# Products of probabilities and values in pairs of steps, with four buffers of probabilities

## Chip, cores and metric

One core of a Trainium2 chip. The metric is the device time of one execution in microseconds. Engines are named as the profile names them: PE is TensorE (matmuls; PEld are its weight loads), DVE is VectorE, ACT is ScalarE, POOL is GpSimd, SP is SyncE, which issues the DMAs.

## The reference

Attention with a bias by relative position that is added after the softmax, two layer norms with residuals, and a layer of 32 small experts of which each token takes its best 4. Four batches of 512 tokens with 128 features, 16 heads of 8.

```
q, k, v = split_heads(x @ Wq), split_heads(x @ Wk), split_heads(x @ Wv)
attn = softmax(einsum('bhqd,bhkd->bhqk', q, k) * e ** -0.5) + bias
x = layernorm(x + layernorm(einsum('bhqk,bhkd->bhqd', attn, v)) * gamma + beta)
sim = (x @ hasher_w.T) @ keys.T
vals, idx = top_k(sim, 4);  w = softmax(vals)
out = sum_k w[k] * (silu(x @ values_down[idx[k]]) @ values_up[idx[k]])
x = layernorm(x + out * scale)
```

## The kernel before

**Rounds and steps.** The kernel runs rounds t = 0 to 4 (2 and, where more are needed, a loop over the middle ones). Round t has the attention of batch t and, from round 1 on, the norms and the experts of batch t - 1; from round 2 on also the last `up` products of batch t - 2. Round 4 is a tail without attention. A round has 16 steps u: four groups of four heads, and in each group four blocks of 128 keys (kc = u % 4). Each engine has its own program, written by hand in a fixed order, and the engines meet at semaphores.

**A step on TensorE** (`round_`, lines 1186 to 1216). Four scores (`scores`, line 1007, bf16, into one of three banks `st_ps`), four maxima matmuls (`maximum_scores`, line 996, into one of two banks `sm_ps`, for the heads seven positions ahead), one product of probabilities and values (`values`, line 1020), and jobs. A product is four matmuls in float32 with 32 columns of weights each, on four column tiles side by side; the trace has eight instructions for it, since each float32 matmul is two passes. It accumulates over the four key blocks of a group in `ov_ps`. In step u stands the product of step u - 1; that of step 15 stands in step 0 of the next round. The order is: score 0 (and 1), maxima m0, scores to 2, maxima m1, the product, maxima m2, jobs "before", score 3, maxima m3, jobs "behind".

**Jobs** (table `JOBS`). Turnings of the shifts for the next group (`shift0` to `shift3`; `shift0` is that of the next round and stands in step 14), of outputs (`o0` to `o3`), of the normed rows (`x1t`, step 5), the expert similarities (`sim`, step 6), the turning of the expert weights `w_tok` (`wt`, step 9), eight `down` and eight `up` products of the experts.

**VectorE** takes the row maximum of each maxima matmul (line 747) in the same order, and between them the normalisation of a head group in steps 1, 5, 9 and 15 (lines 766 and 768), norm statistics in steps 1 to 4, `hid` from step 7 on (line 801) and the ranking of the experts in steps 6 to 9. A maxima matmul waits for the reduction two before it, because there are two banks.

**ScalarE** does the Exp of each score (line 656) into `probs`, of which there are two buffers, so a step's first Exp waits for the product two steps back. It also copies `ov_ps` to `o_sb` after the last product of a group.

**GpSimd** does its work in one queue: copies of values, the norms, the splits of the maxima into three bf16 parts (lines 424 to 431), and the multiplication of `hid` by the expert weights (`weigh`, line 464). The weights `w_rows` reach it from `w_tok` by way of `w_t`, a write to DRAM and eight broadcast reads on SP's queue. The split for `shift0` stands in it behind the sixth of eight multiplications.

Of the kernel before, what the change touches and what calls it, by code (L numbers as in the profile page):

```python
# [5 lines left out]
def bass_postln_attention_product_key_ffn(nc, x, w_q, w_k, w_v, rel_table, gamma, beta,  # L6
# [18 lines left out]
    ALU, ACT, AX = mybir.AluOpType, mybir.ActivationFunctionType, mybir.AxisListType  # L25

    B, S, E = x.shape
    H = rel_table.shape[1]
    D = E // H
    P = 128  # L30
    C = S // P
    J = 4
    G = H // J
    U = G * C
# [11 lines left out]
    LAST = rel_table.shape[0] - 1  # L46
    NWIN = S
    TILE = 32
    EPS_ATTENTION, EPS_LN = 1e-3, 1e-5

    def constant_from(h):

        return min(max(-(-(LAST - S + HPB + HPB * h) // HPB), 0), H)
# [7 lines left out]
    with ctx:  # L61
        def sb(name, shape, dt=F32):
            return ctx.enter_context(nc.sbuf_tensor(name, shape, dt))

        def pb(name, shape, dt=F32):
            return ctx.enter_context(nc.psum_tensor(name, shape, dt))

        def sem(name):
            return ctx.enter_context(nc.semaphore(name))
# [18 lines left out]
        v_all = sb("v_all", [P, C, H, B, D])  # L88
        v_cur = sb("v_cur", [P, C, H, TILE])
        q_stack, k_stack = sb("q_stack", [P, H, S], BF16), sb("k_stack", [P, H, S], BF16)  # L90
# [2 lines left out]
        shift_parts = sb("shift_parts", [P, P // (J * C), J * C], BF16)  # L93
        shift_res = sb("shift_res", [P, J * C])
        shift_rows = sb("shift_rows", [PARTS * J * C, P], BF16)
        probs = sb("probs", [P, 2, J, S])
        o_sb = sb("o_sb", [P, S])
        rsum = sb("rsum", [P, C, J])
        attn = sb("attn", [P, C, E])
        bias_t = sb("bias_t", [P, 2, S])  # L100
        bias_v = sb("bias_v", [P, C, H, B, D])

        z = sb("z", [P, C, E])
# [11 lines left out]
        w_rows = sb("w_rows", [P, FJ, S])  # L115
        tanh_sb = sb("tanh_sb", [P, 3, S])
        hid = sb("hid", [P, FJ, S])
        y, y_out = sb("y", [P, C, E]), sb("y_out", [P, C, E])


        st_ps = pb("st_ps", [P, 3, S])
# [25 lines left out]
        scores_ready, probs_ready, pv_done = sem("scores_ready"), sem("probs_ready"), sem("pv_done")  # L147
# [15 lines left out]
        def maxima_of(u, more):  # L163

            return [(u + LEAD, c) for c in range(C) if more or u + LEAD < U]
# [26 lines left out]
        def here(n, attention, experts, more, late):  # L192

            return (late if n[:2] == "up" else attention if n in OWN else experts) and (more or n != "shift0")
# [42 lines left out]
        def score_bank(k):  # L237


            return 1 if k == U * J - 1 else k % 3  # L240
# [34 lines left out]
        def bias_banks(g):  # L275


            return [(st_ps[:, 0, :], st_ps[:, 2, :]), (st_ps[:, 1, :], st_ps[:, 0, :])][(g - CG) % 2]
# [5 lines left out]
        def is0(t):  # L284
            return isinstance(t, int) and t == 0
# [285 lines left out]
        def _(act):  # L571
# [77 lines left out]
            def exp(t, u, j):  # L649

                n = t * U + u
                act.wait_ge(scores_ready, J * n + j + 1)
                if j == 0 and not (is0(t) and u < 2):

                    act.wait_ge(pv_done, n - 1)
                nc.scalar.activation(probs[:, u % 2, j, :], st_ps[:, score_bank(u * J + j), :], ACT.Exp,  # L656
                                     scale=SCORE_SCALE).then_inc(probs_ready, 1)

            def o_copy(t, g, in_round):
# [294 lines left out]
        def _(pe):  # L954
# [32 lines left out]
            def maximum_scores(t, pos, c):  # L987

                n, h = t * U + pos, pos % U
                k = C * n + c  # L990
                if pos % J == 0 and c == 0:
                    pe.wait_ge(stack_loaded[pos // J % G], 32 * (t + pos // U) + 32)
                if not (is0(t) and pos == 0 and c < 2):

                    pe.wait_ge(max_ready, k - 1)
                nc.tensor.matmul(sm_ps[:, c % 2, :], q_stack[0:SHIFT_ROW, h, c * P:(c + 1) * P],  # L996
                                 k_stack[0:SHIFT_ROW, h, :], start=True, stop=True).then_inc(sm_ready, 1)

            def scores(t, u, j):

                n, g, kc, k = t * U + u, u // C, u % C, u * J + j
                if j == 0 and kc == 0:
                    pe.wait_ge(shift_loaded[g], 16 * t + 16)
                if not (is0(t) and k < 3):

                    pe.wait_ge(probs_ready, J * n + j + 1 - scores_since(k))
                nc.tensor.matmul(st_ps[:, score_bank(k), :], k_stack[:, g * J + j, kc * P:(kc + 1) * P],  # L1007
                                 q_stack[:, g * J + j, :], start=True, stop=True).then_inc(scores_ready, 1)

            def values(t, u):  # L1010

                n, g, kc = t * U + u, u // C, u % C
                if kc == 0:
                    pe.wait_ge(v_ready, t * G + g + 1)
                    if not (is0(t) and g == 0):

                        pe.wait_ge(o_copied, t * G + g)
                pe.wait_ge(probs_ready, J * n + J)
                for j in range(J):
                    i = nc.tensor.matmul(ov_ps[j * TILE:(j + 1) * TILE, :], v_cur[:, kc, g * J + j, :],  # L1020
                                         probs[:, u % 2, j, :], start=(kc == 0), stop=(kc == C - 1))
                i.then_inc(pv_done, 1)

            def turn(dst, src, idn):
# [107 lines left out]
            for kc in range(C):  # L1132
                i = nc.tensor.matmul(st_ps[:, 2, 0:CG * J * B * D], rel_t[:, LAST:LAST + P],
                                     v_all[:, kc, 0:CG * J].rearrange("p h b d -> p (h b d)"),
                                     start=(kc == 0), stop=(kc == C - 1))
# [12 lines left out]
            for g in range(CG, G):  # L1148
                if g >= CG + 2:
                    pe.wait_ge(bias_copied, g - CG - 1)  # L1150
                n = constant_from((g + 1) * J - 1) + 1
                for kc in range(C):
                    for j in range(J):
                        h = g * J + j
                        window = bass.AP(rel_t, S - 1 - HPB * h + (P // H) * kc, [[pitch, P], [HPB, n], [-1, HPB]])
                        i = nc.tensor.matmul(bias_banks(g)[0][j * TILE:(j + 1) * TILE, 0:n * HPB],
                                             v_all[:, kc, h].rearrange("p b d -> p (b d)"), window, start=(kc == 0), stop=(kc == C - 1))
# [18 lines left out]
            def round_(t, attention, experts, more, late):  # L1176
                kind = (attention, experts, more, late)

                def jobs(half):
                    for name in half:  # L1180
                        if here(name, *kind):
                            misc(t, name, kind)

                for u in range(U):
                    before, behind = JOBS.get(u, ([], []))

                    if not attention and u == 0:

                        before, behind = behind, before
                    todo = maxima_of(u, more) if attention else []  # L1190

                    def maxima(k):
                        for pos_c in todo[k:k + 1]:
                            maximum_scores(t, *pos_c)

                    def score(*heads):
                        for j in heads:
                            if attention:
                                scores(t, u, j)

                    spread = not any(here(n, *kind) and n[:2] in ("do", "up") for n in JOBS.get(u - 1, ([], []))[1])
                    score(*range(1 + spread))
                    maxima(0)
                    score(*range(1 + spread, 3))
                    maxima(1)
                    if u and attention:
                        values(t, u - 1)
                    elif u == 0 and experts:
                        values(t - 1, U - 1)
                    maxima(2)  # L1210
                    jobs(before)
                    score(3)
                    maxima(3)
                    jobs(behind)

            rounds(pe, round_)
            for j in range(FJ):
                up(B - 1, j, B + 1)
# [22 lines left out]
```

## Time and profile before

| | |
|---|---|
| time, median of 3 runs | 367.4 us (366.94 to 367.63) |
| span of the profiled execution | 365.1 us |
| busy: PE, DVE, ACT, POOL | 304.6, 239.0, 189.2, 119.1 us |
| TensorE clock granted, mean | 0.922 |
| round 0 from its first product to the first product of round 1 | 51.4 to 99.1 us |
| turning of `w_tok` in rounds 1, 2, 3 | 135.90, 210.18, 283.75 us |

A timeline row has the start and the duration in us, the engine, the line, the operation with its output and inputs, and in brackets how long the engine was idle before it and what ended that. A row with "x4" is four instructions of one kind in a row. Matmuls overlap, so TensorE is best read from start to start.

### The profile page before, as it was taken

The numbers are of one execution on the slowest core, as the hardware profiler recorded it, in microseconds if no ns is written. First come the engines' busy times: TensorE is split into PE (matmuls) and PEld (weight loads), VectorE is DVE, ScalarE is ACT, GpSimd is POOL, SyncE is SP. The second block draws the span as 40 slices with busy tenths as digits, with TensorE's granted clock in tenths as the row PEclk, the third lists the DMA queues.
The fourth block names the chain that finished last, engine by engine and source line by source line (L and its number), as shares of the span: only waits on it lengthen the run. The fifth ranks groups of instructions, "written<-read, shape, count | busy, mean of one in ns | idle before, by whom it ended". The sixth has DMA issues, their size and how long they took to land. (4 is left out here: it accounts for less than half of the span.)

```text
span 365.1 us, 4853 instructions
## 1 busy us (share of the span) xinstructions
PE 304.6 (83%) x1603; PEld 132.9 (36%) x1627; DVE 239.0 (65%) x525; ACT 189.2 (52%) x370; POOL 119.1 (33%) x185
## 2 busy tenths in 40 slices
PE   5858989999998999839999999299999998185771
PEld 2524323232232433214544333145543227142661
DVE  0737797888898798806788988157789222656123
ACT  2634366777776667625466768155567890024000
POOL 8834000011057111450565105513660044440111
PEclk9969999999999999969999999789999999759556
DMA  5487942298112021332021212430000122001220
GB/s 147 96 257 184 309 87 68 75 301 277 40 29 66 5 64 66 110 127 68 3 65 33 65 52 103 137 81 2 1 27 6 45 102 94 0 29 50 103 86 30
DMA packets 32983, 31.83 MB, mean 87 GB/s; under 512 B 6670, under 2 KB 27326, under 8 KB 32958
## 3 DMA queue, kind: packets, MB, share of 16 engines
q1 hardware_dynamic: 32958, 31.52, 29.0%
q8 instruction: 13, 0.21, 0.3%
q14 instruction: 12, 0.10, 0.1%
HBM read 20.57 MB, written 10.78 MB: 86 GB/s over the span
## 5 line engine op out<-in xcount | busy, mean ns | idle before, releaser
L747 DVE TENSOR_REDUCE neg_max<-sm_ps 128x1 f32<-128x512 f32 x256 | 167.4, 685 | 61.5 <-PE sm_ps L996 60.4
L656 ACT ACTIVATE probs<-st_ps 128x512 f32<-128x512 f32 x256 | 137.3, 601 | 46.1 <-PE st_ps L1007 32.2
L996 PE MATMUL sm_ps<-k_stack,q_stack 96*128 96x512 bf16 x256 | 100.2, 393 | 9.4 <-DVE neg_max L747 4.0
L1007 PE MATMUL st_ps<-q_stack,k_stack 128*128 128x512 bf16 x232 | 79.7, 388 | 0.9 <-ACT probs L656 0.7
L1020 PE MATMUL ov_ps<-probs,v_cur 128*32 128x512 f32 x512 | 68.3, 605 | 1.0 <-ACT probs L656 1.0
L996 PEld LDWEIGHTS sm_ps<-k_stack,q_stack 96*128 96x128 bf16 x256 | 24.9, 98 | 100.4 <-DVE neg_max L747 78.7
L464 POOL TENSOR_TENSOR hid<-hid,w_rows 128x512 f32<-128x512 f32 x26 | 33.0, 1268 | 80.9 <-DMA w_rows<-w_dram 80.8
L1041 PE MATMUL si_ps<-up_sb,hid 128*128 128x128 f32 x256 | 39.1, 310 | 10.0 <-DVE hid L939 6.0
L1041 PEld LDWEIGHTS si_ps<-up_sb,hid 128*128 128x128 f32 x256 | 36.4, 219 | 14.0 <-POOL hid L464 5.0
L1007 PEld LDWEIGHTS st_ps<-q_stack,k_stack 128*128 128x128 bf16 x256 | 25.6, 100 | 29.4 <-ACT probs L656 10.4
L1096 PE MATMUL mi_ps<-x_t,down_sb 128*128 128x512 f32 x48 | 24.6, 593 | 0.0
L801 DVE SCALAR_TENSOR_TENSOR hid<-tanh_sb,mi_ps 128x512 f32<-128x512 f32 x24 | 16.3, 680 | 10.6 <-ACT tanh_sb L687 10.6
L687 ACT ACTIVATE tanh_sb<-mi_ps 128x512 f32<-128x512 f32 x24 | 14.4, 600 | 13.6 <-PE mi_ps L1096 13.6
L439 POOL COPY v_cur<-v_all 128x128 f32<-128x128 f32 x16 | 4.5, 291 | 49.8 <-PE ov_ps L1020 49.8
L1020 PEld LDWEIGHTS ov_ps<-probs,v_cur 128*32 128x32 f32 x512 | 10.1, 108 | 23.7 <-issue 18.7
L424 POOL CAST shift_parts<-neg_max 128x16 bf16<-128x16 f32 x16 | 3.2, 197 | 41.5 <-DVE neg_max L747 41.5
L573 ACT ACTIVATE shift_rows<-mi_ps 48x128 bf16<-48x128 bf16 x16 | 4.3, 271 | 22.6 <-PE mi_ps L1025 22.5
L1025 PE MATMUL mi_ps<-ident_bf,shift_parts 128*128 128x128 bf16 x16 | 3.6, 226 | 14.2 <-POOL shift_parts L431 14.0
L939 DVE TENSOR_TENSOR hid<-hid,w_rows 128x512 f32<-128x512 f32 x6 | 4.2, 693 | 16.5 <-DMA w_rows<-w_dram 16.5
L573 ACT ACTIVATE x_t<-si_ps 128x512 f32<-128x512 f32 x4 | 2.4, 597 | 20.1 <-PE si_ps L1025 20.1
L573 ACT ACTIVATE o_sb<-ov_ps 128x512 f32<-128x512 f32 x16 | 9.6, 599 | 5.9 <-PE ov_ps L1020 5.7
L1096 PE MATMUL st_ps<-x_t,down_sb 128*128 128x512 f32 x16 | 9.6, 758 | 0.2 <-DVE hid L801 0.2
(126 smaller groups left out, 268.0 us busy)
## 6 DMA issues: line engine op xcount, KB each, us to landing
w_rows<-w_dram SPq DMA_DIRECT2D x32, 256.0 KB
stack_dram<-parts SPq DMA_DIRECT2D x18, 384.0 KB, 4.7
q_stack<-stack_dram SPq DMA_DIRECT2D x16, 288.0 KB
k_stack<-stack_dram SPq DMA_DIRECT2D x16, 288.0 KB
stack_dram<-parts SPq DMA_DIRECT2D x6, 288.0 KB, 5.0
x_sb<-L_attn_x SPq DMA_DIRECT2D x4, 256.0 KB, 3.5
out<-y_out SPq DMA_DIRECT2D x4, 256.0 KB, 2.5
stack_dram<-parts SPq DMA_DIRECT2D x6, 96.0 KB, 2.1
```

Of the source, the lines that this page charges most:

```text
L439: nc.gpsimd.tensor_copy(v_cur[:, :, g * J:(g + 1) * J, 0:D], v_all[:, :, g * J:(g + 1) * J, t, :]).then_inc(v_ready, 1)
L464: nc.gpsimd.tensor_tensor(hid[:, j], hid[:, j], w_rows[:, j], ALU.mult).then_inc(weighed, 1)
L573: return nc.scalar.activation(dst, src, ACT.Copy, scale=scale)
L656: nc.scalar.activation(probs[:, u % 2, j, :], st_ps[:, score_bank(u * J + j), :], ACT.Exp, scale=SCORE_SCALE).then_inc(probs_ready, 1)
L687: nc.scalar.activation(tanh_sb[:, j % 3, :], down_bank(t, j), ACT.Tanh, scale=0.5).then_inc(act_step, 1)
L747: nc.vector.tensor_reduce(neg_max[:, g % 2, col:col + 1], sm_ps[:, c % 2, :], AX.X, ALU.max, negate=True).then_inc(max_ready, 1)
L801: nc.vector.scalar_tensor_tensor(out=hid[:, j], in0=tanh_sb[:, j % 3, :], scalar=1.0, in1=down_bank(t, j), op0=ALU.add, op1=ALU.mult).then ...
L996: nc.tensor.matmul(sm_ps[:, c % 2, :], q_stack[0:SHIFT_ROW, h, c * P:(c + 1) * P], k_stack[0:SHIFT_ROW, h, :], start=True, stop=True).then ...
L1007: nc.tensor.matmul(st_ps[:, score_bank(k), :], k_stack[:, g * J + j, kc * P:(kc + 1) * P], q_stack[:, g * J + j, :], start=True, stop=True ...
L1020: i = nc.tensor.matmul(ov_ps[j * TILE:(j + 1) * TILE, :], v_cur[:, kc, g * J + j, :], probs[:, u % 2, j, :], start=(kc == 0), stop=(kc == ...
L1041: i = nc.tensor.matmul(si_ps[:, c * P:(c + 1) * P], hid[:, j, c * P:(c + 1) * P], up_sb[:, j, :], start=(j == 0 and c == 0), stop=(j == FJ ...
L1096: i = nc.tensor.matmul(down_bank(t, j), down_sb[:, j * NJ:(j + 1) * NJ, :], x1_t[:], start=True, stop=True)
```

## The change

Products of two steps stand together in the even steps: in step u those of steps u - 2 and u - 1, in step 0 those of steps 14 and 15 of the round before. Odd steps have none. `probs` gets four buffers, so that the first Exp of a step waits for the product four steps back. For its room `bias_t`, used before round 0 only, becomes a part of `hid`.

```
+    AV_STEPS = 2
-        probs = sb("probs", [P, 2, J, S])
+        probs = sb("probs", [P, 2 * AV_STEPS, J, S])
-        bias_t = sb("bias_t", [P, 2, S])
+        bias_t = hid[:, 0:2, :]
...
-                if j == 0 and not (is0(t) and u < 2):
-                    act.wait_ge(pv_done, n - 1)
-                nc.scalar.activation(probs[:, u % 2, j, :], st_ps[:, score_bank(u * J + j), :], ACT.Exp,
+                if j == 0 and not (is0(t) and u < 2 * AV_STEPS):
+                    act.wait_ge(pv_done, n - 2 * AV_STEPS + 1)
+                nc.scalar.activation(probs[:, u % (2 * AV_STEPS), j, :], st_ps[:, score_bank(u * J + j), :], ACT.Exp,
...
-                                         probs[:, u % 2, j, :], start=(kc == 0), stop=(kc == C - 1))
+                                         probs[:, u % (2 * AV_STEPS), j, :], start=(kc == 0), stop=(kc == C - 1))
...
-                    if u and attention:
-                        values(t, u - 1)
-                    elif u == 0 and experts:
-                        values(t - 1, U - 1)
+                    if u % AV_STEPS == 0:
+                        for step in range(AV_STEPS, 0, -1):
+                            if u and attention:
+                                values(t, u - step)
+                            elif u == 0 and experts:
+                                values(t - 1, U - step)
```

TensorE, steps 1 and 2 of round 0, before: `sm_ps` is written by maxima matmuls, `st_ps` by scores, `ov_ps` by the product.

```order
L996 MATMUL sm_ps<-k_stack,q_stack 128x512
L1020 MATMUL ov_ps<-probs,v_cur 32x512 x4
L996 MATMUL sm_ps<-k_stack,q_stack 128x512
L1007 MATMUL st_ps<-q_stack,k_stack 128x512
L996 MATMUL sm_ps<-k_stack,q_stack 128x512
L1007 MATMUL st_ps<-q_stack,k_stack 128x512 x2
L996 MATMUL sm_ps<-k_stack,q_stack 128x512
L1007 MATMUL st_ps<-q_stack,k_stack 128x512
L996 MATMUL sm_ps<-k_stack,q_stack 128x512
L1020 MATMUL ov_ps<-probs,v_cur 32x512 x4
```

The same place in the changed kernel, whose lines stand one further:

```order
L997 MATMUL sm_ps<-k_stack,q_stack 128x512 x2
L1008 MATMUL st_ps<-q_stack,k_stack 128x512
L997 MATMUL sm_ps<-k_stack,q_stack 128x512
L1008 MATMUL st_ps<-q_stack,k_stack 128x512 x2
L997 MATMUL sm_ps<-k_stack,q_stack 128x512
L1008 MATMUL st_ps<-q_stack,k_stack 128x512
L997 MATMUL sm_ps<-k_stack,q_stack 128x512
L1021 MATMUL ov_ps<-probs,v_cur 32x512 x8
```

The product of step 1 is gone, so that m1 and m2 stand side by side, and step 2 has two.

TensorE around the turning of `w_tok`, from m1 of step 9 on, before:

```order
L996 MATMUL sm_ps<-k_stack,q_stack 128x512
L1020 MATMUL ov_ps<-probs,v_cur 32x512 x4
L996 MATMUL sm_ps<-k_stack,q_stack 128x512
L1025 MATMUL mi_ps<-ident_bf,shift_parts 128x128
L1007 MATMUL st_ps<-q_stack,k_stack 128x512
L996 MATMUL sm_ps<-k_stack,q_stack 128x512
L1025 MATMUL si_ps<-ident,w_tok 128x128
```

In the changed kernel:

```order
L997 MATMUL sm_ps<-k_stack,q_stack 128x512 x2
L1026 MATMUL mi_ps<-ident_bf,shift_parts 128x128
L1008 MATMUL st_ps<-q_stack,k_stack 128x512
L997 MATMUL sm_ps<-k_stack,q_stack 128x512
L1026 MATMUL si_ps<-ident,w_tok 128x128
```

The product of step 8 is no longer ahead of the turning; it stands in step 10.

## Rows read from the trace of the kernel before

**Rows 1.** The page: busy time of engines; the costliest groups, TensorE's products.

```profile
PE 304.6 (83%) x1603; PEld 132.9 (36%) x1627; DVE 239.0 (65%) x525; ACT 189.2 (52%) x370; POOL 119.1 (33%) x185
...
L1020 PE MATMUL ov_ps<-probs,v_cur 128*32 128x512 f32 x512 | 68.3, 605 | 1.0 <-ACT probs L656 1.0
```

**Rows 2.** Timeline, round 1: turning of w_tok, GpSimd's wait, TensorE's wait.

```profile
135.90 0.30 PE L1025 MATMUL si_ps<-ident,w_tok 128*128 128x128 f32 x1 [0.16 <-DVE w_tok L895]
...
158.29 1.26 POOL L464 TENSOR_TENSOR hid<-hid,w_rows 128x512 f32<-128x512 f32 x1 [2.28 <-DMA w_rows<-w_dram]
...
160.80 0.27 PE L1025 MATMUL mi_ps<-ident_bf,shift_parts 128*128 128x128 bf16 x1 [6.53 <-POOL shift_parts L431]
```

**Rows 3.** Timeline, tail: VectorE's variance, GpSimd's last multiplication and its norm.

```profile
306.25 0.38 DVE L786 BATCH_NORM_AGGREGATE mv<-stats 128x2 f32<-128x6 f32 x4
...
310.81 1.26 POOL L464 TENSOR_TENSOR hid<-hid,w_rows 128x512 f32<-128x512 f32 x1 [1.32 <-DMA w_rows<-w_dram]
...
312.15 0.23 POOL L448 TENSOR_SCALAR veps<-mv 128x4 f32<-128x4 f32 x1
```

**Rows 4.** Timeline, round 0, a plain step: TensorE, then VectorE.

```profile
83.57 0.61 PE L1020 MATMUL ov_ps<-probs,v_cur 128*32 128x512 f32 x4
84.12 0.39 PE L996 MATMUL sm_ps<-k_stack,q_stack 96*128 96x512 bf16 x1
84.34 0.38 PE L1007 MATMUL st_ps<-q_stack,k_stack 128*128 128x512 bf16 x1
...
85.89 0.39 PE L996 MATMUL sm_ps<-k_stack,q_stack 96*128 96x512 bf16 x1
86.21 1.06 PE L1020 MATMUL ov_ps<-probs,v_cur 128*32 128x512 f32 x8
87.21 0.39 PE L996 MATMUL sm_ps<-k_stack,q_stack 96*128 96x512 bf16 x1
...
84.54 2.48 DVE L747 TENSOR_REDUCE neg_max<-sm_ps 128x1 f32<-128x512 f32 x4 [0.61 <-PE sm_ps L996]
87.64 2.54 DVE L747 TENSOR_REDUCE neg_max<-sm_ps 128x1 f32<-128x512 f32 x4 [0.61 <-PE sm_ps L996]
```

**Rows 5.** Timeline, round 1, VectorE in steps 2 to 4.

```profile
106.94 3.08 DVE L747 TENSOR_REDUCE neg_max<-sm_ps 128x1 f32<-128x512 f32 x5
110.60 2.48 DVE L747 TENSOR_REDUCE neg_max<-sm_ps 128x1 f32<-128x512 f32 x4 [0.57 <-PE sm_ps L996]
113.34 0.87 DVE L778 BATCH_NORM_STATS2 stats<-z 128x6 f32<-128x128 f32 x4 [0.25 <-POOL z L528]
```

**Rows 6.** Timeline, rounds 1 and 2, steps 15, 1, 3, 4 and 8.

```profile
164.09 0.69 DVE L747 TENSOR_REDUCE neg_max<-sm_ps 128x1 f32<-128x512 f32 x1 [1.44 <-PE sm_ps L996]
...
165.75 0.39 PE L996 MATMUL sm_ps<-k_stack,q_stack 96*128 96x512 bf16 x1
...
172.75 0.69 DVE L747 TENSOR_REDUCE neg_max<-sm_ps 128x1 f32<-128x512 f32 x1 [0.40 <-PE sm_ps L996]
...
174.08 0.39 PE L996 MATMUL sm_ps<-k_stack,q_stack 96*128 96x512 bf16 x1
...
182.03 1.34 DVE L747 TENSOR_REDUCE neg_max<-sm_ps 128x1 f32<-128x512 f32 x2 [0.64 <-PE sm_ps L996]
...
183.58 0.39 PE L996 MATMUL sm_ps<-k_stack,q_stack 96*128 96x512 bf16 x1
...
188.19 1.29 DVE L747 TENSOR_REDUCE neg_max<-sm_ps 128x1 f32<-128x512 f32 x2
...
204.02 0.39 PE L996 MATMUL sm_ps<-k_stack,q_stack 96*128 96x512 bf16 x1
...
205.07 0.69 DVE L747 TENSOR_REDUCE neg_max<-sm_ps 128x1 f32<-128x512 f32 x1
```

**Rows 7.** Timeline, round 0, VectorE in steps 5 and 15 to 0.

```profile
64.92 3.14 DVE L747 TENSOR_REDUCE neg_max<-sm_ps 128x1 f32<-128x512 f32 x5
...
98.81 0.69 DVE L747 TENSOR_REDUCE neg_max<-sm_ps 128x1 f32<-128x512 f32 x1 [0.23 <-PE sm_ps L996]
```

## The prediction

> **What bounds the kernel now.** The page comes first: TensorE is busy 83% of the span and VectorE 65%, and the products of probabilities and values are 512 of TensorE's instructions, eight to a step [rows 1]. A total does not say what sets the end, so the second view is the timeline at the two places where work ends that everything else waits for. In the last step but one of a round with experts, TensorE sits idle 6.53 us until GpSimd has split the next shifts. GpSimd could not, for its queue stood behind a multiplication by `w_rows` that waited for a DMA, and that DMA goes back to the turning of `w_tok` in step 9, at 135.90 [rows 2]. So from step 9 to the split the time is that of DMAs: what TensorE does in steps 10 to 14 costs nothing, up to those 6.53 us. In the tail it is the same: the mean and variance of the last batch are there at 306.63, but GpSimd takes them at 312.15, behind the multiplication that the last-but-one slice of `w_rows` released [rows 3]. **The path** is thus round 0 from step 1, round 1 to step 9, then steps 15 and 0 to 9 of rounds 2 and 3. The rest hangs on those three `w_tok`.
>
> What limits a step on the path? I read a plain one of round 0 in the timelines of both engines [rows 4]. TensorE issues the step's second maxima matmul (call it m1) at 85.89, the product at 86.21, the third one (m2) at 87.21; VectorE starts on m2 at 87.64, 0.43 later. Reductions in a row start 0.60 apart ((2.48 - 0.69)/3). The next m1 may go only when the reduction two before it has ended, since there are two banks: 0.60 + 0.69 after VectorE took m2, and 0.05 of semaphore. The loop is 1.32 + 0.43 + 0.60 + 0.69 + 0.05 = 3.09, which is the distance from one m2 to the next (84.12 to 87.21). It is a chain through both engines, and the product stands inside it: while it runs VectorE idles 0.61 [rows 4].
>
> **The change, part by part.**
>
> *The even steps, each with one more product.* One product is two passes of four matmuls. From its start to m2 it is 1.00 (86.21 to 87.21), from its second pass to m2 0.55 (83.57 to 84.12), so the passes are 0.45 apart, and of the 1.00 two passes are 0.91 and 0.09 stands behind them [rows 4]. No row shows two products in a row. I take 0.91 for the second, two passes without the 0.09; the bounds are 0.88 (four pitches of 0.22, that of two bf16 matmuls of 512 columns, 84.12 to 84.34) and 1.10 (it starts afresh, 1.00 and 0.10 ahead of it). m2, and with it VectorE, comes 0.91 later. Even steps on the path: 2, 4, ... 14 in round 0, and 0, 2, 4, 6, 8 in each of rounds 1 to 3, so 7 + 15 = 22, or +20.0 us.
>
> *Cover.* Where VectorE has other work queued when m2 comes, part of the 0.91 is hidden. In step 2 of round 1 it runs behind until 106.94 and starts on m2 some 0.60 later, so 0.37 is hidden; in step 4 of round 1 it is held by a statistic that waits for GpSimd's `z`, 0.46; in step 4 of rounds 2 and 3 m1's reduction starts at 188.19 and the next at 188.80, where m2 issued about 188.20 was ready at 188.62, so 0.2 each; in step 8 of all three rounds m2 goes at 204.02 and is taken at 205.07 only, so 0.63 each [rows 5, 6]. With 0.05 each in step 2 of rounds 2 and 3: 0.37 + 0.46 + 0.4 + 1.9 + 0.1 = 3.2 us. Net of the even steps: +16.8.
>
> *The odd steps, without a product.* m2 follows m1 at once, but it has to wait for the reduction of m0. The step is then VectorE's: four reductions 0.60 to 0.61 apart, 2.45 in place of 3.09, a gain of 0.64 and not of the product's 1.00. That holds in steps 1, 3, 7, 11 and 13 of round 0: 3.2 us. In steps 5 and 9 the normalisation of a head group stands between the reductions, and VectorE has five in a row with no idle time behind it, so nothing is gained; in step 15 only the 0.23 of idle time ahead of the next step, with the overlap of 0.07: 0.3 [rows 7]. In round 1, step 1 is full of normalisation and statistics up to 106.94 (nothing), step 3 gives back its 0.57 and the overlap (0.64), step 5 waits for GpSimd's norm (nothing), and in steps 7 and 9 VectorE works without a gap on reductions, `hid` and the ranking (nothing) [rows 5]. In rounds 2 and 3, m2 could go 0.74 after m0's reduction starts: in step 15 at 164.83 and not 165.75, in step 1 at 173.49 and not 174.08 (0.59), in step 3 at 182.77 and not 183.58 (0.81) [rows 6]. Of the 0.92 of step 15 I count 0.6, since m3 then waits for m1's reduction, which ends late (bounds 0.26 and 0.92). Steps 5, 7 and 9 give nothing, as in round 1. Together 3.5 + 0.64 + 2 x 2.0 = 8.1 us.
>
> *Edits with no price.* Four buffers of probabilities: the Exp of a step waits for a product four steps back. With pairs it was done one or two steps before, so ScalarE is not held, nor SP and GpSimd. `bias_t` in the place of `hid`: one is used before round 0, the other first written in round 1. The product of step 8 goes from ahead of `w_tok`'s turning to behind it; that turning waits for VectorE's `w_tok`, not for the product. The copies of `ov_ps` stand one to four steps, as before, behind the last product of a group. Steps 10 to 14 change by 1 to 2 us, inside the 6.53 of [rows 2]; if that cover were gone, they would add 3 us in all.
>
> **The sum.** +16.8 - 8.1 = +8.7. The profiled execution: 365.1 + 8.7 = 373.8. The median lies 2.3 above the span, so 367.4 + 8.7 = 376.1 us.
>
> **A rule beside the rows.** The product runs on column tiles of 32, all else on the whole array, and a change between the two costs: 0.09 behind the product, and 0.32 from m1 to it where the pitch is 0.22, so 0.10 ahead [rows 4]. The Trainium skill, TensorEngine Tiling (Array Packing), section Key Properties, says it: "Changing tiling mode (not just tile) drains the TensorE". The trace agrees, with 0.19 a product. By that rule alone half the switches go and the kernel gets faster, which is the first rival; its price comes from the rows.
>
> **The rivals.**
> *TensorE is the limit, and each switch saved is time saved.* For it: TensorE is the busiest engine [rows 1], and two of the odd steps of rounds 2 and 3 give back most of what its work is shorter by [rows 6]. The path now holds 15 + 10 + 11 + 11 = 47 products at 1.00 + 0.10; it would hold 22 pairs at 1.10 + 0.91 (three products move behind `w_tok`). That is 51.7 less 44.2, so 367.4 - 7.5 = 359.9 us. It decides if m2 can go right behind m1 in an odd step, that is if m0's reduction has ended by then. Against it: m0 goes 0.44 ahead of m1, and its reduction ends 0.43 + 0.69 after its issue, 0.46 after the place of m2; and in the plain step VectorE idles while TensorE multiplies.
> *A seam between the products.* If the second starts afresh it costs 1.10 and not 0.91, 22 times 0.19: +4.2, 380.3 us. Against: the second pass of a product follows the first at 0.45, its weights loaded beneath, and the next product is on the same four tiles.
> *VectorE catches up better.* If the even steps of rounds 1 to 3 hide another 0.3 each (15 times) since VectorE arrives with more queued from the odd step, 4.5 is saved: 371.6 us. Against: it is never more than two reductions behind, by the two banks.
> *The path is elsewhere,* in transfers that do not go back to `w_tok`: then nothing changes, 367.4 us. Against: the turning of `w_tok` waited 0.16 for VectorE alone, and GpSimd's multiplication for the DMA of what it made [rows 2].
>
> **How the numbers follow.** Chances: the forecast (372.5 to 379) 0.70, the seam (379 to 382) 0.08, the better cover (369 to 372.5) 0.10, the path elsewhere 0.04, TensorE the limit 0.08. Measurements of this kernel tell about 0.2% from no change. The range takes in the forecast, most of the better cover and part of the seam: 370.5 to 380.5. Faster 0.08, the same 0.04, slower 0.88.
>
> **What would show it.** In the timeline after: 16 instructions of the product in a row, m2 1.91 behind their start in even steps; in plain pairs of round 0, products 6.4 apart (2 x 3.09 + 0.91 - 0.64) where two steps took 6.18; VectorE idle 1.5 before m2 of an even step and not at all in the odd one; the idle time of TensorE until the shift split near 6 us again; from `w_tok` to the end the same time as now. The three turnings of `w_tok` should come about 5.3, 7 and 8.7 later. I am wrong if the pairs of round 0 are no further apart than 6.18, or if the reductions of the odd steps do not follow each other without a gap.

## The result, and the profile after

The changed kernel takes **374.19 us** (median of 4 runs, 372.99 to 375.05) beside 367.51 for the kernel before (4 runs). The ratio is **1.019, 95% interval 1.015 to 1.022**: slower by 6.7 us. The forecast was 376.1 and its range 370.5 to 380.5. The profiled execution took 372.99, its span is 371.2.

These are the page's busy times and the two groups that changed most, of the kernel after (a row: busy us, mean ns, then idle time just before and what ended most of it):

```profile
PE 303.3 (82%) x1604; PEld 134.6 (36%) x1627; DVE 238.0 (64%) x525; ACT 189.9 (51%) x370; POOL 118.9 (32%) x185
...
L748 DVE TENSOR_REDUCE neg_max<-sm_ps 128x1 f32<-128x512 f32 x256 | 166.1, 683 | 68.5 <-PE sm_ps L997 67.7
...
L997 PE MATMUL sm_ps<-k_stack,q_stack 96*128 96x512 bf16 x256 | 99.7, 391 | 21.5 <-DVE neg_max L748 14.8
```

And the same two groups on the page of the kernel before:

```profile
L747 DVE TENSOR_REDUCE neg_max<-sm_ps 128x1 f32<-128x512 f32 x256 | 167.4, 685 | 61.5 <-PE sm_ps L996 60.4
...
L996 PE MATMUL sm_ps<-k_stack,q_stack 96*128 96x512 bf16 x256 | 100.2, 393 | 9.4 <-DVE neg_max L747 4.0
```

The two busiest engines have no more to do: TensorE 303.3 us against 304.6, VectorE 238.0 against 239.0 [rows 1]. But VectorE waits 7 us longer for TensorE's maxima, and TensorE's maxima wait 11 us longer for VectorE (14.8 against 4.0, the part that VectorE's reductions end). Each engine now waits for the other at different times. That is a loss without a culprit in the totals; it is seen only in the order of things within a pair of steps. The timeline of the kernel after, round 0, steps 2 to 4, TensorE first:

```profile
52.59 0.39 PE L997 MATMUL sm_ps<-k_stack,q_stack 96*128 96x512 bf16 x1
52.91 1.92 PE L1021 MATMUL ov_ps<-probs,v_cur 128*32 128x512 f32 x16
54.77 0.39 PE L997 MATMUL sm_ps<-k_stack,q_stack 96*128 96x512 bf16 x1
...
57.14 0.39 PE L997 MATMUL sm_ps<-k_stack,q_stack 96*128 96x512 bf16 x1 [0.20 <-DVE neg_max L748]
...
59.25 1.06 PE L1021 MATMUL ov_ps<-probs,v_cur 128*32 128x512 f32 x8
```

then VectorE:

```profile
43.34 10.43 DVE L748 TENSOR_REDUCE neg_max<-sm_ps 128x1 f32<-128x512 f32 x17 [0.25 <-PE sm_ps L997]
55.20 4.97 DVE L748 TENSOR_REDUCE neg_max<-sm_ps 128x1 f32<-128x512 f32 x8 [1.43 <-PE sm_ps L997]
61.53 1.29 DVE L748 TENSOR_REDUCE neg_max<-sm_ps 128x1 f32<-128x512 f32 x2 [1.37 <-PE sm_ps L997]
```

m2 comes 1.86 behind the start of the two products (52.91 to 54.77), where it came 1.00 behind one [rows 4]: the second product costs 0.86. VectorE idles 1.43 before it, then does eight reductions with no gap, through the whole odd step; that is why the odd step gives nothing like 1.00 back. The pair takes 6.34 us (52.91 to 59.25) where two steps took 6.18.

The other reading is TensorE's wait before the shift split, and the turning of `w_tok` in rounds 1 and 2:

```profile
139.55 0.30 PE L1026 MATMUL si_ps<-ident,w_tok 128*128 128x128 f32 x1 [0.16 <-DVE w_tok L896]
```

```profile
164.42 0.27 PE L1026 MATMUL mi_ps<-ident_bf,shift_parts 128*128 128x128 bf16 x1 [4.00 <-POOL shift_parts L432]
```

```profile
215.45 0.30 PE L1026 MATMUL si_ps<-ident,w_tok 128*128 128x128 f32 x1 [0.16 <-DVE w_tok L896]
```

The turning is 3.65 later in round 1 (135.90 before [rows 2]), 5.27 in round 2, 6.08 in round 3. From the turning to the split it is 24.87 us, where it was 24.90: that stretch swallowed its pairs, and the wait at its end shrank from 6.53 [rows 2] to 4.00. By stretch, with the start of the first score matmul and the turnings as marks:

| us | before | after |
|---|---|---|
| start to first score | 47.93 | 46.98 |
| first score to turning 1 | 87.97 | 92.57 |
| turning 1 to split 1, turning 2 to split 2 | 24.90, 25.24 | 24.87, 24.43 |
| split 1 to turning 2, split 2 to turning 3 | 49.38, 48.33 | 51.03, 49.95 |
| turning 3 to end | 81.35 | 81.37 |

The path, that is the second and fourth lines, grew by 4.60 + 1.65 + 1.62 = 7.9 us. The span grew by 6.1, because this execution had its first score 0.95 sooner and one stretch of transfers 0.8 shorter. The first says little: two kernels below that have the four buffers and no pair before step 12 of round 1 had their first score at 47.17 and 48.49, on either side of the kernel before. For the second no run tells whether the change has a part in it.

### The profile page after: what moved, and what is told of

Same layout as the page of the kernel before. It is cut to its first block and busy times, and to the rows that moved or that the text cites. A ratio compares the mean times of both kernels' runs of the same rounds, so it can differ in the third digit from the quotient of the medians.

```text
span 371.2 us, 4852 instructions
## 1 busy us (share of the span) xinstructions
PE 303.3 (82%) x1604; PEld 134.6 (36%) x1627; DVE 238.0 (64%) x525; ACT 189.9 (51%) x370; POOL 118.9 (32%) x185
## 5 line engine op out<-in xcount | busy, mean ns | idle before, releaser
L997 PE MATMUL sm_ps<-k_stack,q_stack 96*128 96x512 bf16 x256 | 99.7, 391 | 21.5 <-DVE neg_max L748 14.8
L1021 PE MATMUL ov_ps<-probs,v_cur 128*32 128x512 f32 x512 | 61.6, 598 | 0.0
L1021 PEld LDWEIGHTS ov_ps<-probs,v_cur 128*32 128x32 f32 x512 | 13.4, 109 | 29.4 <-issue 17.8
L574 ACT ACTIVATE o_sb<-ov_ps 128x512 f32<-128x512 f32 x16 | 9.6, 598 | 17.4 <-PE ov_ps L1021 17.4
```

Source lines behind the costliest of these rows:

```text
L574: return nc.scalar.activation(dst, src, ACT.Copy, scale=scale)
```

## The experiments

All are compared with runs of the kernel before on the same chip. A plain step or pair below is one of round 0 with nothing but reductions on VectorE.

**Only the buffers.** Does the loss come from the four buffers or from `bias_t` in the place of `hid`? The kernel before with those edits alone (`AV_STEPS` is 2):

```
-        probs = sb("probs", [P, 2, J, S])
+        probs = sb("probs", [P, 2 * AV_STEPS, J, S])
...
-        bias_t = sb("bias_t", [P, 2, S])
...
+        bias_t = hid[:, 0:2, :]
...
-                if j == 0 and not (is0(t) and u < 2):
-                    act.wait_ge(pv_done, n - 1)
-                nc.scalar.activation(probs[:, u % 2, j, :], ...
+                if j == 0 and not (is0(t) and u < 2 * AV_STEPS):
+                    act.wait_ge(pv_done, n - 2 * AV_STEPS + 1)
+                nc.scalar.activation(probs[:, u % (2 * AV_STEPS), j, :], ...
```

> The four buffers of probabilities and bias_t in hid alone; the products stand as before, one in each step. Theory (VectorE is starved while two products run): buffers cost nothing, 367.4 us as before, within 0.3%. Rival (the memory, the longer distance between Exp and product, or the alias costs): 370 us or more, a part of the 6.7 us.

366.82 us (10 runs) against 367.08 (25 runs), ratio 1.000, interval 0.998 to 1.003. The buffers are free; the loss is all in where the products stand.

**One product in the even steps, none in the odd ones.** The changed kernel without the first product of each pair, to split the sum into its two halves:

```
                     if u % AV_STEPS == 0:
-                        for step in range(AV_STEPS, 0, -1):
-                            if u and attention:
-                                values(t, u - step)
-                            elif u == 0 and experts:
-                                values(t - 1, U - step)
+                        if u and attention:
+                            values(t, u - 1)
+                        elif u == 0 and experts:
+                            values(t - 1, U - 1)
```

Two more edits, not shown, go with it: a sum over key blocks begins at the first product that is left, and each product counts as two at its semaphore.

> The changed kernel with the first product of each pair left out (half of the products of probabilities and values are not computed): even steps have one product, odd steps none. It splits the sum. Theory: against the changed kernel it is faster by what the second product costs net of cover, 22 x 0.86 less 3.2 = 16 us, so 358 us; against the kernel before it is faster by what the odd steps give back, 8 to 9 us, and not by the 25 products x 1.10 us = 27 us that are gone from the path. Rival (TensorE's own work is the limit): 340 us.

The median of ten runs is 364.3 us, ratio 0.992 (0.989 to 0.994): by the medians the 358 us expected were missed. The profiled run is the fastest, 359.3. The others lie between 361.4 and 367.5 at a mean granted clock of 0.893 to 0.916, where this one had 0.924 and the kernel before 0.917 to 0.930. On the three stretches of the path its clock was 1.00, 0.96 and 0.94 and that of the kernel before 1.00, 0.96 and 0.96, so the trace of this run is what is compared; what follows rests on this one execution. Its TensorE in the same steps:

```profile
52.76 1.06 PE L1021 MATMUL ov_ps<-probs,v_cur 128*32 128x512 f32 x8
53.76 0.39 PE L997 MATMUL sm_ps<-k_stack,q_stack 96*128 96x512 bf16 x1
...
56.13 0.39 PE L997 MATMUL sm_ps<-k_stack,q_stack 96*128 96x512 bf16 x1 [0.21 <-DVE neg_max L748]
...
58.24 1.06 PE L1021 MATMUL ov_ps<-probs,v_cur 128*32 128x512 f32 x8
```

and its VectorE:

```profile
54.18 4.96 DVE L748 TENSOR_REDUCE neg_max<-sm_ps 128x1 f32<-128x512 f32 x8 [0.57 <-PE sm_ps L997]
```

With half of all products gone a plain pair takes 5.48 (52.76 to 58.24), 0.70 less than two steps before, and VectorE again has eight reductions in a row. A whole product out of the odd step is worth 0.70 there, not 1.00. The path's three stretches are 84.09, 48.18 and 47.15, so **emptying the odd steps gave back 3.9 + 1.2 + 1.2 = 6.3 us**; and from there to the changed kernel, **the second products cost 8.5 + 2.9 + 2.8 = 14.1**. If TensorE were the limit, this kernel would have come near 340.

**Pairs only where time was said to be free.** The kernel before with the four buffers, and with pairs in steps 12 and 14 of rounds 1 to 3 alone (steps 11 and 13 have no product then):

```
+                    paired = experts and attention
+                    if paired and u in (12, 14):
+                        values(t, u - 2)
+                        values(t, u - 1)
+                    elif paired and u in (11, 13):
+                        pass
+                    elif u and attention:
...
```

> Pairs only in steps 12 and 14 of rounds 1 to 3, which lie behind the turning of w_tok; all other steps as before. Theory (the path ends at w_tok, the DMAs and GpSimd set the time from there to the shift split): 367.4 us, the same, and TensorE's wait before the split changes by under 1 us. Rival (a step costs what it takes wherever it stands): 6 of 22 pairs, +2 us or more.

367.37 us against 367.08, ratio 1.000 (0.998 to 1.003): the stretch behind `w_tok` hides its pairs. What was missed is the size of what it hides:

```profile
161.14 0.26 PE L1026 MATMUL mi_ps<-ident_bf,shift_parts 128*128 128x128 bf16 x1 [4.68 <-POOL shift_parts L432]
```

It was 6.53 [rows 2]. A pair takes 8.22 here (its products start at 145.99 and 154.21) where two steps took 7.40 (138.08 to 145.48 in the kernel before), so two pairs spent 1.64 of it. What a plain pair of round 0 costs (6.34 less 6.18) does not hold in these steps: each also has two matmuls of the experts' first layer (`down`) on TensorE, and the `hid` made of them on VectorE, and the odd step without a product is no shorter for it. VectorE now waits 0.94 ahead of m2 and still 0.44 in the next gap, as the rows of these two engines in the first of the two pairs show:

```profile
145.99 1.92 PE L1021 MATMUL ov_ps<-probs,v_cur 128*32 128x512 f32 x16
...
154.21 1.92 PE L1021 MATMUL ov_ps<-probs,v_cur 128*32 128x512 f32 x16
```

```profile
148.27 1.29 DVE L748 TENSOR_REDUCE neg_max<-sm_ps 128x1 f32<-128x512 f32 x2 [0.94 <-PE sm_ps L997]
150.00 0.69 DVE L748 TENSOR_REDUCE neg_max<-sm_ps 128x1 f32<-128x512 f32 x1 [0.44 <-PE sm_ps L997]
150.61 0.68 DVE L802 SCALAR_TENSOR_TENSOR hid<-tanh_sb,mi_ps 128x512 f32<-128x512 f32 x1
```

**The two products apart.** In an even step one product behind m1 and one behind m3, so that VectorE never starves for two at a time:

```
-                        for step in range(AV_STEPS, 0, -1):
-                            if u and attention:
-                                values(t, u - step)
...
+                        if u and attention:
+                            values(t, u - 2)
...
+                    if u % AV_STEPS == 0:
+                        if u and attention:
+                            values(t, u - 1)
```

> Every second step has two products, as in the changed kernel, but apart: one after the second maxima matmul, one after the fourth (in the tail together). Theory (VectorE starves at each block of products, since no more than two maxima are under way): in a plain pair of steps VectorE idles 0.6 at the first and 1.0 at the second, 6.5 us a pair where the changed kernel takes 6.34 and the kernel before 6.18; with four switches of tiles and not two in each pair the whole is as slow as the changed kernel or slower, 374 to 378 us. Rival (the long block itself is the harm, and two short ones are hidden): back near 368 us.

390.41 us, ratio 1.066 (1.061 to 1.070): far outside what either theory said. A plain pair did what was expected, 6.47 (82.39 to 88.86). The rest I read as another coupling; no run moved the copy on which it hangs. In steps 4, 8, 12 and 0 ScalarE copies `ov_ps` behind the last product of a head group. ScalarE, then TensorE in step 12 of this kernel:

```profile
91.75 0.60 ACT L574 ACTIVATE o_sb<-ov_ps 128x512 f32<-128x512 f32 x1 [2.18 <-PE ov_ps L1021]
```

```profile
90.62 1.06 PE L1021 MATMUL ov_ps<-probs,v_cur 128*32 128x512 f32 x8
...
92.89 0.39 PE L1008 MATMUL st_ps<-q_stack,k_stack 128*128 128x512 bf16 x1 [0.45 <-ACT probs L657]
```

The copy stands where it stood in ScalarE's queue, but its product came later; ScalarE waited 2.18 us with the Exps of the step queued behind, and TensorE then waited for these. The pair that begins with such a copy one group earlier, 74.10 to 82.39, took 8.29 where it takes 7.40 in the changed kernel. Over the kernel ScalarE idles 35.9 us ahead of that copy, 17.4 in the changed kernel:

```profile
L574 ACT ACTIVATE o_sb<-ov_ps 128x512 f32<-128x512 f32 x16 | 9.6, 597 | 35.9 <-PE ov_ps L1021 35.9
```

So the place right behind m1 seems not to be a free choice in this kernel, and this experiment says nothing on a product's own price.

**VectorE out of the way.** Both kernels with the reductions over 128 of the 512 columns of each bank; the rest is not looked at, which the maximum is then without. The same edit, line 747 or 748:

```
-                nc.vector.tensor_reduce(neg_max[...], sm_ps[:, c % 2, :], AX.X, ALU.max,
+                nc.vector.tensor_reduce(neg_max[...], sm_ps[:, c % 2, 0:P], AX.X, ALU.max,
```

The kernel before:

> The kernel before with each reduction of a maxima matmul over 128 of its 512 columns (the maximum of three quarters of the keys is left out), so that VectorE is quick. A reduction should take about 0.3 us and not 0.69. Theory: a plain step is then TensorE's, 8 x 0.217 + 1.10 = 2.83 us and not 3.09; the whole 355 to 361 us.

The changed kernel:

> The changed kernel with the same short reductions. Theory (the pair is slower only because VectorE and its two banks cannot keep up in the odd step): now it is not slower; a plain pair of steps takes 2 x 1.74 + 1.96 + 0.1 = 5.55 us where the kernel before with short reductions takes 5.66, and the whole is 1 to 6 us faster than that one. Rival (two products together, or the missing work between them, cost time of themselves): 5 us or more slower than the kernel before with short reductions.

358.66 us (ratio 0.976, 0.973 to 0.978) and 357.73 (0.976, 0.972 to 0.979). **With a reduction of 0.29 us in place of 0.68 the 6.7 us are gone**, and the path's stretches of the two add up alike to 0.1 us. The rows of TensorE before and after, with short reductions:

```profile
60.59 1.06 PE L1020 MATMUL ov_ps<-probs,v_cur 128*32 128x512 f32 x8
...
66.89 0.64 PE L1020 MATMUL ov_ps<-probs,v_cur 128*32 128x512 f32 x4
```

```profile
55.47 0.61 PE L1008 MATMUL st_ps<-q_stack,k_stack 128*128 128x512 bf16 x2 [0.51 <-DMA q_stack<-shift_rows]
...
56.66 1.92 PE L1021 MATMUL ov_ps<-probs,v_cur 128*32 128x512 f32 x16
```

The changed kernel was expected to be 1 to 6 us the faster one here, the switches saved now being on the path. It was only as fast. The pairs of steps 10 to 12 and 12 to 14 take 5.65 and 5.64 where the same steps take 5.68 and 5.69, so two products in a row spare 0.03 to 0.05, not 0.19. The three early pairs are longer: 6.30, 6.43 and 6.12 where the same steps take 5.74, 6.30 and 5.74. In the first of them the shift rows, which are now turned behind the pair, come late, the row above; the others are open.

**A longer stretch on the path.** The last test was of the split. If GpSimd splits the next shifts ahead of its fourth multiplication by `w_rows` and not behind the sixth, TensorE's 6.53 us should go, and with them the cover of steps 10 to 14. The edit, on the kernel before:

```
-                    for j in range(FJ // 2) if attention else TAIL_POOL:
+                    for j in range(FJ // 2 - 1) if attention else TAIL_POOL:
...
-                        fetch_values(t + 1, 2)
+                        split_shift(t + 1, 0)
...
-                        for j in range(FJ // 2, FJ - 2):
-                            weigh(f, t, j)
+                        weigh(f, t, FJ // 2 - 1)
...
-                        split_shift(t + 1, 0)
+                        fetch_values(t + 1, 2)
...
-                        for j in range(FJ - 2, FJ):
+                        for j in range(FJ // 2, FJ):
```

> The kernel before with one edit on GpSimd: the split for shift0 of the next round stands ahead of the fourth multiplication by w_rows in place of behind the sixth. Theory (the path leaves TensorE at the turning of w_tok only because that split stands behind a multiplication that waits for a DMA): TensorE's waits of 6.5 and 6.9 us before the split fall below 1 us and its clock does not fall behind them (up to 2 us more each), 352 to 356 us. Rival (something else is due at the same time, w_rows or a slice of the next round): 362 us or more.

370.61 us, ratio 1.009 (1.007 to 1.012): slower, where 352 to 356 was expected. TensorE no longer waits for the split, but it waits five scores further on:

```profile
154.97 0.22 PE L1024 MATMUL mi_ps<-ident_bf,shift_parts 128*128 128x128 bf16 x1
...
167.72 1.03 PE L1006 MATMUL st_ps<-q_stack,k_stack 128*128 128x512 bf16 x2 [8.61 <-DMA q_stack<-shift_rows]
```

The queue of SyncE, which issues the loads, in the same place:

```profile
149.60 2.45 SPq L399 DMA_DIRECT2D w_rows<-w_dram  x1
152.16 2.41 SPq L313 DMA_DIRECT2D q_stack<-stack_dram  x1
154.62 1.82 SPq L313 DMA_DIRECT2D k_stack<-stack_dram  x1
156.49 0.78 SPq L319 DMA_DIRECT2D q_stack<-shift_rows  x1
```

The shift rows are 12 KB. Issued at 156.49, they are there only at 167.7, 11 us later, behind eight loads of `w_rows` of 256 KB each and two slices of 288 KB; GpSimd waited for the last `w_rows` until 165.22. In the changed kernel with short reductions, in round 0 and with no large load under way, such rows issued at 53.00 were there at 55.47. So GpSimd's order is not all that ends the stretch behind `w_tok`: with it out of the way, the transfers that `w_tok` sets off do. That they hold the small one back because they share its queue is how I read it; no run moved it to another.

The same edit on the changed kernel:

> The changed kernel with the same edit. Steps 10 to 14 are now on the path, and there a pair takes 8.22 us where two steps took 7.40. Theory: 362 to 367 us, 8 to 13 us slower than the kernel before with this edit, where the pairs alone cost 6.7. Rival (the pairs are harmless where TensorE has down products to do): no more than 7 us slower than that one.

380.97 us, ratio 1.038 (1.033 to 1.044), where 362 to 367 was expected. By the medians the pairs cost 10.4 us here and not 6.7: 8 to 13 was expected. TensorE's wait for the shift rows shrinks to

```profile
170.49 1.04 PE L1007 MATMUL st_ps<-q_stack,k_stack 128*128 128x512 bf16 x2 [6.10 <-DMA q_stack<-shift_rows]
```

The difference has the size that was expected, but the traces do not bear out its reason (steps 10 to 14 come onto the path). The wait shrank from 8.61 to 6.10, by the 2.5 us that the pairs take there, so they are still covered. And the two profiled executions differ by 6.4 us only (376.9 against 370.5): from first score to first turning the pairs cost 4.63, between turnings 1.23 and 1.84, where it was 4.60, 1.62 and 0.81 without this edit. Where the medians get the other 4 us from is open. Neither kernel is faster than the one before, and no version that does all the work was found that beats it.

## Why the prediction was right

**What bounds the kernel: right.** The path does leave TensorE at `w_tok`. From turning to split, and from the third turning to the end (81.37 against 81.35), nothing grew, and pairs in that stretch alone are free.

**The mechanism: right.** The odd step is VectorE's and gives back part of a product. VectorE idles 1.43 before m2 (said: 1.5) and not at all in the odd step; step 1 gave 0.65 (said: 0.64); with VectorE's work cut the loss is gone. m2 comes 1.86 behind the pair's start (said: 1.91).

**The second product: 0.05 too much, and outside the bounds.** I took 0.91 and a lower bound of 0.88; it is 0.86. Over 22 pairs that is 1.1 us.

**Its cover: 1.6 too small.** 22 x 0.86 = 18.9, of which 14.1 arrived, so 4.8 was hidden and not 3.2. In round 0 nothing was hidden: the pairs with one normalisation grew by 0.79, but that is 0.86 less 0.07 that the odd step gave back. What was missed is GpSimd's: 0.8 more in step 2 of rounds 2 and 3 each and 0.6 more in step 4 of round 1, both below, against 0.5 less in the three steps 8.

**The odd steps: 1.8 too much.** 6.3 and not 8.1. In step 3 of rounds 2 and 3 I had counted 0.81 each. With that product gone VectorE runs into the next thing, a statistic of `z` for which GpSimd is late. VectorE in that step of the kernel with one product a pair, of the changed kernel and of the kernel before:

```profile
179.11 0.87 DVE L779 BATCH_NORM_STATS2 stats<-z 128x6 f32<-128x128 f32 x4 [1.37 <-POOL z L529]
```

```profile
188.57 0.87 DVE L779 BATCH_NORM_STATS2 stats<-z 128x6 f32<-128x128 f32 x4 [0.56 <-POOL z L529]
```

```profile
185.36 0.88 DVE L778 BATCH_NORM_STATS2 stats<-z 128x6 f32<-128x128 f32 x4 [0.66 <-POOL z L528]
```

From the products of step 2 (at 171.56, 181.02 and 177.79) to this statistic it is 7.55, 7.55 and 7.57 us: the norm on GpSimd sets the time there. So what step 2 loses this wait absorbs, and what step 3 wins it takes back. The pair moved by +0.01 in round 2 and +0.03 in round 3; I said +0.05, but by two large terms of which neither shows. The failed step is the cover of 0.05 that I gave step 2 of these rounds, and with it the 0.81 of step 3: I had counted the norm's wait in round 1 only.

In round 1 it is the same, in step 4. Step 2 to 4 came out at -0.18 (said -0.10) and 4 to 6 at +0.44 (said +0.45), but not by the terms that I gave: from step 2 to the statistic it is 7.58 to 7.59 in all three kernels, and all that the change adds up to step 6 stands behind it, 0.26.

**Step 8: mis-sized.** I hid 0.63 of each, by the time that VectorE took m2 late. From the products of step 8 to the turning it grew by 0.53 in round 1 and 0.52 in round 2, and not by 0.28; in round 3 by 0.26. TensorE has the turning of outputs and an expert matmul behind the last maximum of that step, and in the kernel before it had waited only 0.39 for VectorE:

```profile
205.01 0.39 PE L996 MATMUL sm_ps<-k_stack,q_stack 96*128 96x512 bf16 x1 [0.39 <-DVE neg_max L747]
```

Cover has to be read on the engine on which the chain goes on.

**TensorE's wait before the split: wrong.** "Near 6 again" against 4.00 and 3.57. I let steps 10 to 14 change by 1 to 2 us. With the experts' matmuls in the steps a pair adds 0.82, and the three pairs of these steps took 2.5. It cost nothing here, and the effect on the end was said rightly; had the wait of the kernel before been under 2.5 us, it would have cost.

**The sum.** It said +16.8 - 8.1 = +8.7; the runs say +14.1 - 6.3 = +7.8, two terms too large by about as much. That the net came out so well is luck, and no sign that its terms do. The three turnings were said 5.3, 7 and 8.7 later and came 3.65, 5.27 and 6.08 later, of which 0.95 is the earlier start and, for the third, 0.8 the shorter transfer.

**The rivals.** TensorE as the limit (359.9) is excluded by the two kernels with half of the products and with short reductions; a seam (380.3) by the 0.86. A better cover (371.6) came true in part of its size, 1.6 of 4.5 us, but not by its reason: behind steps 0 and 6, where VectorE also comes from an odd step, the second product costs its full 0.85 to 0.87, and what is hidden more is behind GpSimd's norm. The path elsewhere (367.4) is excluded by the 6.7 us and by the pairs that are free behind `w_tok`.

The Trainium skill, TensorEngine Tiling (Array Packing), Key Properties, says that a change of tiling mode drains TensorE. The trace agrees: two products in a row take 1.86 and not twice 1.00. But a saved switch is worth time only where TensorE is what the next one waits for, and even with short reductions the plain pair became only 0.03 to 0.05 shorter.

## What to carry to other kernels

Putting two blocks of an engine's work together saves the switch between them and lengthens the one gap that its consumer sees. Count what the consumer has queued (here reductions 0.60 us apart from two banks) against the longer block: if it is less, the whole second block is on the path. What the emptied place gives back is bounded by that consumer, and by the next thing it depends on; read that, on the engine where the chain continues, before counting it.

An order that is moved on one engine moves the due times of all that read its results: when one product went later, ahead of a copy on ScalarE that kept its place, the kernel took 16 us more than the changed one; that the copy is the cause is read from the trace, not tested.

## What the runs showed of the hardware

- Two blocks of eight column-tiled matmul instructions in a row take 1.86 us to the next matmul, one takes 1.00; the second is below four pitches of 0.22.
- With 256 of the products' 512 instructions left out the mean granted clock was lower, not higher, 0.893 to 0.916 in nine of ten runs, against 0.917 to 0.930 in the kernel before. Less work on TensorE did not mean a better clock. Why one run kept 0.924 is open.
- A load of 12 KB took 11 us to land with eight loads of 256 KB and two of 288 KB ahead of it, and 2.5 us with no large load under way.
